# Edge groups of 8, thirty times 16 and 10 pairs; a quad of sums first in each slot of TensorE

## What is computed

```python
feat_all = jnp.einsum('ni,rhid->rnhd', inputs, conv_weights)      # every node under every type
el = jnp.sum(feat_all[edge_type, edge_src] * attn_l[edge_type], axis=-1)
er = jnp.sum(feat_all[edge_type, edge_dst] * attn_r[edge_type], axis=-1)
e = jax.nn.leaky_relu(el + er, negative_slope=0.2)
ex = jnp.exp(e - jax.ops.segment_max(e, edge_dst)[edge_dst])
alpha = ex / jax.ops.segment_sum(ex, edge_dst)[edge_dst]
h = jax.ops.segment_sum(alpha[..., None] * feat_all[edge_type, edge_src], edge_dst)
```

## Time and profile before

| | |
|---|---|
| median of 3 runs | 2463.84 us (2459.18 to 2472.21) |
| profiled execution | 2463.08 us |
| its span | 2461.3 us |
| mean granted TensorE clock | 0.799 |
| TensorE, VectorE, ScalarE, GpSimd busy | 78%, 46%, 35%, 47% |
| gathers of the edge stage | 996 |

### The profile page before, as it was taken

The page is one execution under the profiler, slowest core; times in us unless marked ns, Lnnn a source line. Parts: engine busy times, 40 slices in busy tenths (PEclk is TensorE's granted clock), DMA queues, the critical chain, the costliest instruction groups (busy, mean ns, idle before and its releaser), DMA issues. The chain is left out here.

```text
span 2461.3 us, 34365 instructions
## 1 busy us (share of the span) xinstructions
PE 1913.0 (78%) x9138; PEld 1610.3 (65%) x9139; DVE 1129.8 (46%) x3075; ACT 865.2 (35%) x2347; POOL 1145.3 (47%) x1164
## 2 busy tenths in 40 slices
PE   8999233677877777787776878678688689999998
PEld 7887133555666566666555666556566678999887
DVE  6332022456655555556555655556567632212211
ACT  2222122343433343333333343344446532222221
POOL 4000744656665656565565665556540453222222
PEclk9999555777776778767876786777788689999999
DMA  6443422333333333333333333333322777877774
GB/s 239 191 170 143 109 60 70 93 85 89 91 92 88 87 87 96 87 89 86 88 91 87 88 93 88 89 86 93 86 60 77 268 245 213 254 243 248 242 234 104
DMA packets 121155, 315.49 MB, mean 128 GB/s; under 512 B 27047, under 2 KB 71335, under 8 KB 106180
## 3 DMA queue, kind: packets, MB, share of 16 engines
q0 software_dynamic: 60192, 149.24, 23.4%
q1 hardware_dynamic: 60836, 164.88, 19.5%
HBM read 257.36 MB, written 57.71 MB: 128 GB/s over the span
## 5 line engine op out<-in xcount | busy, mean ns | idle before, releaser
L787 POOL DMA_INDIRECT gath<-feats,idxT x996 | 953.5, 957 | 811.2 <-issue 285.9
L1137 PE MATMUL psP<-gath,hot 128*128 128x260 f32 x1992 | 677.5, 495 | 88.7 <-issue 51.3
L1137 PEld LDWEIGHTS psP<-gath,hot 128*128 128x128 f32 x1992 | 466.6, 246 | 193.3 <-issue 109.4
L1034 ACT COPY hotT<-psOT 128x512 f32<-128x512 f32 x249 | 144.5, 580 | 887.3 <-remote 689.0
L1096 PE MATMUL psOT<-cst,hot 128*128 128x128 f32 x996 | 204.7, 343 | 320.8 <-ACT hotT L1034 211.2
L1096 PEld LDWEIGHTS psOT<-cst,hot 128*128 128x128 f32 x996 | 151.3, 178 | 375.6 <-issue 344.7
L1121 PEld LDWEIGHTS psE<-er,hotT 128*128 128x128 f32 x1992 | 313.9, 238 | 42.2 <-issue 38.5
L903 DVE TENSOR_TENSOR acc<-acc,psP 128x260 f32 x498 | 210.9, 424 | 275.0 <-remote 151.3
L1121 PE MATMUL psE<-er,hotT 128*128 x1992 | 310.7, 306 | 27.4 <-DVE er_e L818 23.8
L1024 ACT ACTIVATE hot<-cst,ndlT 128x128 f32<-128x128 f32 x996 | 317.4, 393 | 4.7 <-PEq L325 4.7
L894 DVE TENSOR_TENSOR gath<-gath,psA 128x1024 f32<-128x1024 f32 x241 | 291.5, 1220 | 10.0 <-ACT gath L1062 2.9
(11 more groups left out here) (232 smaller groups left out, 1183.7 us busy)
## 6 DMA issues: line engine op xcount, KB each, us to landing
w1buf<-in_experts SPq DMA_DIRECT2D x43, 1030.0 KB
w2buf<-in_experts SPq DMA_DIRECT2D x43, 1024.0 KB
feats<-frow SPq DMA_DIRECT2D x29, 1040.0 KB, 3.9
gath<-feats,idxT POOLq DMA_INDIRECT x996
meta<-in_edges SPq DMA_DIRECT2D x464, 12.0 KB
acc<-slots_x SPq DMA_DIRECT2D x23, 258.0 KB
gath<-in_b SPq DMA_DIRECT2D x43, 128.0 KB
acc<-slots_x SPq DMA_DIRECT2D x20, 129.0 KB
```

The lines of the kernel that those rows point to most:

```text
L787: pool.indirect_dma_start(gath[:, r, u], None, feats, bass.IndirectOffsetOnAxis(ap=idxT[:, r, u:u + 1], axis=0)).then_inc(gath_in[r], 16)
L1034: act.copy(hotT[:, j % 2], psOT[:]).then_inc(hotT_copied, 1)
L1137: ins = pe.matmul(psP[:, bank(g, b, r), 0:FW], hot[:, r, u], gath[:, r, u], start=u % BLK == 0, stop=u % BLK == BLK - 1)
```

## The change

The first group has 8 pairs in place of 4, the last 10 in place of 14. The sums of a slot stand at its start in place of its end, so turn, right logits and (in slot 5) the transposes of the records come behind them. Nothing else differs.

```diff
--- before.py
+++ after.py
@@ -49,7 +49,7 @@
 GB = 16
 GU = GB * BLK
 assert GU * HEADS == P
-SIZES = [4] + [GB] * ((PAIRS - 18) // GB) + [14]
+SIZES = [8] + [GB] * ((PAIRS - 18) // GB) + [10]
 SHORT = GB - SIZES[0]
 GROUPS = len(SIZES)
 BASES = [sum(SIZES[:g]) for g in range(GROUPS)]
@@ -1185,6 +1185,10 @@
                         return
 
                     def slot(s):
+                        if s < SLOTS_Q - LAG:
+                            total(g - 1, (r - 1) % GBUFS, s + LAG)
+                        else:
+                            total(g, r, s - (SLOTS_Q - LAG))
                         if s + 2 < SLOTS_Q:
                             turn(g + 1, (r + 1) % GBUFS, s + 2)
                         else:
@@ -1193,10 +1197,6 @@
                             right_logits(g + 1, s + 1)
                         if s == 5 and there(g + AHEAD):
                             meta_rows(g + AHEAD)
-                        if s < SLOTS_Q - LAG:
-                            total(g - 1, (r - 1) % GBUFS, s + LAG)
-                        else:
-                            total(g, r, s - (SLOTS_Q - LAG))
 
                     pe.wait_ge(e_ready, g + 1)
                     pe.transpose(psS[:, S_ET:S_ET + P], e_sb[:, 1], ident).then_inc(eT_ready, 1)
```

## The result

The changed kernel takes 2554.22 us (median of 4 runs, 2549.93 to 2559.89) against 2466.71 (4 runs, 2459.18 to 2472.21): a ratio of 1.034, 95% interval 1.0312 to 1.0367. It is slower by 87.5 us, where the prediction had it 22 us faster. Its profiled execution took 2554.86 us around a span of 2553.1, at a mean granted clock of 0.796 (0.799 before).

A forecast was written before the change was run, and what follows sets the result against it. No engine is full; a chain of gather series, late answers and VectorE's steps sets the 50.6 us period. 2463.1 - 27 (27 periods at -1.0) + 5 (sizes) = 2441 us; overall range 2390 to 2555.

The forecast's parts named there:

- Ahead of zero: Before the late copy, counted as 0: quads 3 and 4 both summed, so GpSimd's pause of 2.03 us goes.
- Spread to pick: From spread to VectorE's pick of right logits: spread ends 3.4 us or more earlier; pick could start at +8.2.
- Pick to gathers: From VectorE's pick to GpSimd's next gathers: -1.0 us a period taken, between -1.5 at best and +6.5.
- the row at 1799.90: Trace case of 12 gathers for quads 3 to 5, pick in time; next series 17.89 us later; basis of -1.0.
- R3 held: Rival: quad 3's right logits answered only at the series' end; +6.5 us a period, 2644 us in all periods; chance 0.25.
- the turn of 1033.40: Sign of late answers: TensorE's turn recorded inside 12 gathers, taking 1.06 us, copied by ScalarE only at 1043.59.
- Behind the shift: After the shift, up to the records' transposes: 4.5 us of delay hidden by a cover of 7 us, counted 0.
- a second pause that goes: Rival: GpSimd goes on from quads 6 and 7 into the next group; -4.1 us a period, 2357 us; chance 0.12.
- No change in the period: Rival: the pause that goes comes back as a longer one behind the 12 gathers; 2468 us; chance 0.25.
- Start: First gather series grows from 72 to 80; group 0's maxima at about 360 against 344.57: +15 us, +8 to +22.
- End: Last group: fewer gathers, sums, turns and right logits shorten the tail; -10 us, from 0 to -12.
- The rule weighed: TensorE's clock drops in waits; quad 4's sums filling the old wait would keep 2.4 GHz: 2430 rather than 2441 us.

The follow-up runs named there:

- slots01_only: Kernel before with old sizes and sums first in slots 0 and 1 alone; late chip: 2512.44 against 2493.63 us, +0.75%.
- mix_e: Old sizes, four parts in one kernel: new order, slot 2 old, old order, new order with GpSimd's pause kept; late chip: 2511.09 against 2490.51 us for before.
- after_third: The changed kernel once more, unedited, against the kernel before on another late chip: 2543.85 against 2490.62 us, +2.1%.
- The pause: Changed kernel with GpSimd's gather of quad 4 waiting for one more sum, the first half of quad 5; prompt chips: ratios to before 1.0021 and 1.0027.

## Why the prediction was wrong

*Ahead of zero* held: quads 3 and 4 are both summed, and GpSimd's stop between them, at 1051.33 in the earlier trace rows, is gone. *Spread to pick*, first half, held: 3.6 us gained where I had 3.4.

*Pick to gathers* is the step that failed first. I took -1.0 us a period, near the row at 1799.90 where a pick had come in time beside 12 gathers. The runs showed R3 held to the end of whatever series it was recorded in: a series of 8 in most periods, with the next gathers at +19.9 for +19.7, and one of 12 in seven, at +25.6. Against before that is +5.9, where my rival "R3 held" had +6.5, in seven periods of 26 and not in half. The row at 1799.90 was one instance, from the end of the stage, and I let it outweigh the turn of 1033.40; the pick itself had waited four times, 25.1 us, in the trace of before. Nor was it like the steady period: S5 was recorded there from 1802.78 for 2.00 us, so until 4.9 us into the series in place of 7.1, and SyncE had issued the last record load of the stage by 1751.86. That rival had the mechanism, but put it on R3's place behind S5; by slots01_only and mix_e the merged series holds the pick with R3 ahead of S5 as well, for a smaller loss. What also failed is that S5 would be answered early enough for 12 in every period: its record ends 7.1 us into the series both at 1088.38 and at 1191.62, and only the second series went on to 12, the one with no record load beside it.

*Behind the shift*, counted at 0 by a cover of 7 us, was the second. The cover holds in a common period, where GpSimd stops anyway, but before had four periods without that stop, in which the transposes came 0.3 us behind the gap; at 3.4 us behind it (1169.61) the next stop is there. With the fifth short period, at the end of the stage, that is 30 us. I had named a second pause that goes as a rival for after, and had not looked for it in before.

*No change in the period* fell for late chips (51.9 and more against 51.1) and holds for prompt ones, by another bound: GpSimd's issue.

*Start*: first maxima at 360.30, where I had 360; by group 3 the 15.7 us are 12.7. *End*: of -10 only the tail's -3.3 (22.1 us from the chain of group 31 to the end of the stage, 25.4 before) is there, and 1.6 are lost between groups 29 and 31; net -1.7. Sizes together +11, where I had +5, within its bounds. So 2463.1 + 79.0 + 10.9 + 1.9 = 2554.9, the profiled execution.

*The rule weighed.* S5 at 1091.61 took 3.84 us, so TensorE was at 1.2 GHz behind the turn's wait of 2.02 us though S4 stood ahead of it. S4 itself stood still between its matmuls, for 0.73 us ahead of 1083.92 and 1.72 us ahead of 1086.01. My sum's side of that choice was right, and R3 came at +7.7 from the turn. The sums behind the new waits of 6.11 and 11.93 us took 3.45 and 3.73 us where a warm quad takes 2.00. That agrees with the Trainium skill, "TensorE: Matmul & The Clock Gate", section "HAM oscillation — how this bites in real kernels": bursts behind a wait begin cold. In the common period this cost nothing by itself, as the next gathers waited for VectorE first. But the clock is part of the seven long periods: each stands behind an S7 that ran at 1.2 GHz and that GpSimd waited for. My sum had no term for it, and what it is worth alone no run shows.

**What stays open.** Why some chips hold answers and others don't; why S7 runs at 1.2 GHz in seven periods of 26 after and in four before; whether SyncE's record loads hold S5's answer or only stand beside it (in after_third they had ended by +2.1 us six times, and no series went on to 12); and how the loss divides between the held pick and the late index columns on a late chip. The pause was not run on a late chip as a kernel of its own. Of the sizes on a late chip I have the trace of after, no kernel of their own.

## What to carry to other kernels

A pause of an engine is not always lost time: here GpSimd's pauses were the moments in which other engines' answers came out, and merging two series took one away. Before an early sum is put ahead, ask what the engine that it frees will start, and what will then wait for its end. And look for the exceptional periods, of the kernel before (five of 45.3 us here) and of the row that a forecast leans on: a delay that the common period hides may be what they can't bear, and a row from the end of a stage may lack an engine's work that the steady period has.

## What the runs showed of the hardware

One program, unchanged, takes 2081 to 2087 us on five chips and 2467 to 2494 in four other measurements. The rows differ in one thing that I could find: whether what TensorE finishes inside a series of gathers is answered at once (copy at 996.70 behind a turn recorded from 996.00 to 996.66) or, in most cases, up to 2.2 us behind the end of the series (1208.65 above). Late chips too answer some inside a series: S5, recorded until 1198.69, let GpSimd go on at 1201.70 without a stop. And GpSimd itself, when it stands in a wait between two gathers, is let go at once (0.04 us behind S7, at 620.80 and 1165.48). The pitch of the gathers is 1.26 us on both. Three rounds on one chip give an interval of 0.1% and say nothing of the other kind: the change is +0.2% on one and +3.4% or +2.1% on the other.
